# Layer 0 of a four-layer attention kernel: four small matrix-product steps 0.0265 of a beat later in TensorE's order, and the first steps of an item's end 0.06 of a beat later

## What is computed

```python
q = einsum('oc,bct->bot', Wq, x) + bq;  k = ... kv ...;  v = ... kv ...      # bs=8, c=256, t=512
attn = softmax(where(kv_mask, einsum('bhqd,bhdk->bhqk', q / sqrt(d), k), -inf))
mean = einsum('bhqk,bhkd->bhqd', attn, v)
ex2  = einsum('bhqk,bhkd->bhqd', attn, v * v)
std  = sqrt(relu(ex2 - mean * mean))
xn   = (x - mean_t(x)) / sqrt(relu(var_t(x)) + 1e-5)                       # masked, over t
out  = (xn * std + mean) * mask
```

## Time and profile before

| | us |
|---|---|
| median of 3 runs | 3299.74 (3284.89 to 3302.26) |
| the profiled execution's own time | 3297.55 |
| its span, first to last instruction | 3295.8 |
| mean granted clock of TensorE | 0.923 of full speed |
| busy: PE, DVE, ACT, POOL (share of the span) | 2809.2 (85%), 1824.8 (55%), 1338.8 (41%), 881.5 (27%) |

### The profile page before, as it was taken

The page is one execution under the profiler, slowest core; times in us unless marked ns, Lnnn a source line. Parts: engine busy times, 40 slices in busy tenths (PEclk is TensorE's granted clock), DMA queues, the critical chain, the costliest instruction groups (busy, mean ns, idle before and its releaser), DMA issues. The chain is left out here.

```text
span 3295.8 us, 41359 instructions
## 1 busy us (share of the span) xinstructions
PE 2809.2 (85%) x14624; PEld 1317.3 (40%) x14624; DVE 1824.8 (55%) x4498; ACT 1338.8 (41%) x2342; POOL 881.5 (27%) x722
## 2 busy tenths in 40 slices
PE   4988888867999999989999999985668888888895
PEld 1222222224555555556555545542222333333332
DVE  3777777713433433212555665567867776667641
ACT  0566665642333333322333333322215544554562
POOL 1577777752444444310010000001110010101000
PEclk7999999978999999899999999988678899999997
DMA  4444444320002000122323232333333232323210
GB/s 99 102 100 102 102 99 102 67 95 23 27 30 92 28 27 24 65 63 56 67 53 69 57 70 52 70 63 86 67 82 87 69 76 59 89 52 77 66 34 20
DMA packets 182335, 219.93 MB, mean 67 GB/s; under 512 B 40840, under 2 KB 135664, under 8 KB 175984
## 3 DMA queue, kind: packets, MB, share of 16 engines
q1 hardware_dynamic: 170064, 189.74, 25.0%
q0 software_dynamic: 6016, 20.98, 1.9%
q10 hardware_dynamic: 6048, 6.56, 0.6%
HBM read 146.90 MB, written 51.64 MB: 60 GB/s over the span
## 5 line engine op out<-in xcount | busy, mean ns | idle before, releaser
L1260 DVE TENSOR_REDUCE l_M<-PS 128x1 f32<-128x512 f32 x512 | 330.2, 681 | 168.3 <-PE PS L722 167.9
L1480 DVE TENSOR_REDUCE l_M<-PS 128x1 f32<-128x512 f32 x512 | 334.8, 684 | 139.1 <-PE PS L967 136.2
L1199 ACT ACTIVATE l_P<-PS 128x512 f32<-128x512 f32 x512 | 286.3, 599 | 255.3 <-PE PS L977 237.3
L1563 POOL TENSOR_TENSOR l_S<-l_P 128x512 f32<-128x512 f32 x256 | 326.0, 1305 | 62.0 <-ACT l_P L1050 62.0
L1050 ACT ACTIVATE l_P<-PS 128x512 f32<-128x512 f32 x512 | 276.3, 598 | 134.0 <-PE PS L731 133.5
L967 PE MATMUL PS<-l_KS,l_QS 97*128 97x512 bf16 x512 | 205.4, 412 | 102.9 <-DVE l_M L1480 71.7
L1319 DVE TENSOR_REDUCE l1a_M<-PS 128x1 f32<-128x512 f32 x256 | 158.9, 683 | 201.5 <-PE PS L784 201.5
L1164 ACT ACTIVATE l_P<-l_P 128x1024 f32<-128x1024 f32 x128 | 135.3, 1057 | 304.9 <-DVE l_P L1400 304.7
L1386 DVE CUSTOM_DVE_ANT_0 l_JK<-PS,l_MK 128x256 f32<-128x256 f32 x512 | 195.6, 420 | 102.1 <-PE PS L897 99.9
L722 PE MATMUL PS<-l_KS,l_QS 97*128 97x512 bf16 x512 | 202.5, 406 | 57.7 <-DMA l_KS<-l_MB 19.5
L612 PE MATMUL PS<-l_YT,l_w_mlp_w 128*128 128x256 f32 x1024 | 238.6, 390 | 5.2 <-ACT l_YT L1126 5.1
(11 more groups left out here) (244 smaller groups left out, 4639.8 us busy)
## 6 DMA issues: line engine op xcount, KB each, us to landing
l_QS<-q_scratch SPq DMA_DIRECT2D x128, 128.0 KB, 5.6
q_scratch<-l_T SPq DMA_DIRECT2D x96, 128.0 KB
l_QS<-q_scratch SPq DMA_DIRECT2D x32, 384.0 KB, 5.0
k_scratch<-l_T SPq DMA_DIRECT2D x96, 128.0 KB
l_KS<-k_scratch SPq DMA_DIRECT2D x32, 384.0 KB
l_QS<-q_scratch SPq DMA_DIRECT2D x32, 256.0 KB, 5.6
l_KS<-k_scratch SPq DMA_DIRECT2D x32, 256.0 KB
l_RB<-l_recs SPq DMA_DIRECT2D x32, 256.0 KB
```

Of the source, the lines that this page charges most:

```text
L1199: e.activation(t.P[quad % 4][:, m, :], PS[:, COUNTS.bank[st], :], ACT.Exp, scale=0.25).then_inc(q.sem("act.exp", st), 1)
L1260: e.tensor_reduce(t.M[i % 2][:, qt, hd:hd + 1], PS[:, COUNTS.bank[st], :], AX.X, ALU.max).then_inc(q.sem("dve.smax", st), 1)
L1480: e.tensor_reduce(t.M[i % 2][:, qt, hd:hd + 1], PS[:, COUNTS.bank[st], :], AX.X, ALU.max).then_inc(q.sem("dve.smax", st), 1)
L1563: x = e.tensor_tensor(t.S[j % 2][:, m, :], t.P[2 * j % 4][:, m, :], t.P[(2 * j + 1) % 4][:, m, :], ALU.add)
```

## The change

Two due times move, in layer 0 alone. The sums go from 0.8625 + n/4 to 0.889 + n/4. The steps f1 0, f1 1 and f2 go from 0.08, 0.16 and 0.28 to 0.14, 0.22 and 0.34. No instruction is added, removed or altered, no delay in `LATER` is changed, and the order within the rings stays as it was.

```diff
         for n in range(4):
-            out += [(0.51 + n / 4, k("fold", n)), (0.8625 + n / 4, k("sums", n))]
+            out += [(0.51 + n / 4, k("fold", n)), (0.889 + n / 4, k("sums", n))]
...
         if h:
-            out += [(0.08, k("f1", 0)), (0.16, k("f1", 1)), (0.28, k("f2")), (1.2, k("f3", 0)), (1.25, k("f3", 1)),
+            out += [(0.14, k("f1", 0)), (0.22, k("f1", 1)), (0.34, k("f2")), (1.2, k("f3", 0)), (1.25, k("f3", 1)),
```

## The result

The changed kernel takes 3280.5 us in the median (3267.7 to 3289.7) where the kernel before takes 3299.4 on the same chip: a ratio of 0.9943, with a 95% interval of 0.9925 to 0.9960, so 18.8 us less (13 to 25). The prediction was 3281. The profiled execution took 3280.75 us, its span is 3279.0. So the time came out as forecast. Whether it came out so for the reasons given is another question, and the experiments answer it with yes for the largest term and for v 0, and no for proj 1.

A forecast was written before the change was run, and what follows sets the result against it. TensorE was taken as the bound, a pair of beats being set by its own order and then the chain through SP; 13.2 + 3.2 + 2.1 = 18.5 us off gave a median of 3281, 8-in-10 range 3265 to 3300.

The forecast's parts named there:

- Proj 0 in the odd beat: Odd beat: proj 0 1.00 us earlier, its evacuation by DVE 1.20 more; 2.2 us in six beats, 13.2 us.
- SP's queue as almost gapless: Odd beat: SP's DMAs from q's write at 396.29 to RB at 426.79 follow with almost no gap.
- the chain: From the odd beat's proj 0 through SP's DMAs to RB and the maxima; the even beat's stalls hang on it.
- One sign: Even beat: RB should arrive about 2 us earlier after proj 0.
- TensorE's lead and the price of f1: Odd beat: TensorE gains 1.3 us of lead; f1 1 beside POOL costs up to 0.7 us six times, taken as 0.
- V 0: Every beat: the 0.53 us wait for v 0's bank goes; it pays in six even beats, 3.2 us.
- Proj 1: Even beat, at 0.sq: proj 1 goes ahead of sums 2, 0.7 us earlier; 2.1 us, bounds 0 and 4.2.
- The clock did not come back: Rival, chance 0.13: the shorter stall behind 0.sq no longer lowers TensorE's clock; 8.4 us more, 3273.
- ACT held at the sums: Slower rival, chance 0.13: the sums' copy delays ACT's next exponential, 16.0 to 19.2 us over 32 copies; 3316 to 3319.
- The condition named for it: The slower rival decides once ACT's 0.90 us idle time is used up, and if the chain's gain fails too.
- What was costed at nothing: Sums 0 after v 1, f2 behind fold 3, f1 of the last batch: nothing, since no stall hangs on them.

The follow-up runs named there:

- first term alone: Against the kernel before: f1 and f2 moved as in the change, and of the sums only sums 1 of the odd beats; 0.9949, 16.8 us off.
- the sums of the first half alone: Against the kernel before: only sums 1 to 3 of the even beats and sums 0 of the odd ones moved; 0.9959, 13.5 us off.
- Three small delays of due times: Changed kernel with the sums' copy on ACT at 0.05, f3 0 at 1.235 and f3b 0 at 1.335; 0.9861 of before, 3255.8 us.

## Why the prediction was right, and where it was not

*Proj 0 in the odd beat (13.2 us): right.* The steps moved as worked out: proj 0 ahead of sums 1, the evacuation right behind ACT's copy, the third write of q at 6.52 us (6.8 foretold). Tried alone, the term gave 16.8 us (11 to 23), and its pair 2.43 us where 2.2 was foretold. Behind it the reading of SP's queue as almost gapless was too kind: between 396.29 and 426.79 it stands for 9.4 us, in four gaps, but each lies ahead of a DMA that reads what the DMAs just before it wrote, so the gaps move with the chain. One sign was worded wrongly: I wanted RB some 2 us earlier "after proj 0". Of the 2.2 us one is proj 0's own, so from proj 0 only 1.20 can be seen; RB's DMA goes 37.05 us after proj 0 in the mean of the last five odd beats, before 38.16: 1.1 earlier.

The prediction cut a pair in two: from the end of the stall behind 0.sq to the next odd proj 0 by TensorE's own order, and from there to the end of the next such stall by the chain. Both can be read off the starts of these matmuls (means of the same four pairs, us):

| | TensorE's own stretch | the chain's stretch |
|---|---|---|
| before | 21.80 | 59.23 |
| first term alone | 20.88 | 57.72 |
| changed | 20.27 | 58.44 |
| foretold for the change | 1.53 less (sums 1 1.00, v 0 0.53) | 1.55 less (f1 1.20, proj 1 0.35) |
| measured for the change | 1.53 less | 0.79 less |

*TensorE's lead and the price of f1: right.* The stall behind f1 1 came back in part, 0.52 to 0.77 us in the last five odd beats. f1 0 went from 1.07 to 1.46 us there, which I had not counted, f1 1 from 0.68 to 1.20, inside the 0.7 that I had set as its bound. With the first term alone the pair is 2.43 us shorter, so neither has taken anything from it that shows.

*V 0 (3.2 us): right, as far as one execution tells.* TensorE's own stretch is shorter by what was foretold, 1.53 us: 0.92 of it comes with the first term alone, and 0.61 more with the rest of the sums.

*Proj 1 (2.1 us): the stall went as foretold, the gain didn't stay.* The chain's stretch, where it should show, is 0.72 us longer than with the first term alone. Single pairs of either kernel scatter there by 2 to 3 us, so the size is loose; the waits and the rows of proj 1 in 145 to 605 us say where it goes. The changed kernel wins 6.1 us behind 0.sq. It loses 4.6 on the maxima (1.0 to 5.6), 5.6 on proj 1's bank (0.9 to 6.5), and proj 1 takes 4.7 us longer (23.8 to 28.5). The 5.8 won at v 0 belong to the own stretch in the even beats, and in the odd ones to a lead that the chain was foretold to take back. So the step "0.7 us on what sets the end of the stall" failed, with its bound of nothing below: I costed what an earlier proj 1 gives to the square roots, and not what the same step takes away, namely that sums 2 filled the wait for the bank and kept TensorE busy ahead of proj 1. With sums 2 put back, proj 1 is at 615 ns again and no loss of time shows. The medians, 16.8 (11 to 23) and 18.8 us off (13 to 25), are too close to tell.

*The clock did not come back.* The rival let it, for 8.4 us. The stalls behind 0.sq did get shorter, 2.7 to 2.9 us for 3.4 to 4.0, but behind each of the six vals still take 1.93 or 1.94 us, and after the one at 442.06 a small matmul takes 0.61, as in the earlier trace rows. On the other side proj 1 fell to the lower level in three even beats, which no rival had. The mean granted clock of 145 to 552 us, 0.94 for 0.96, is no measure of that: it was 0.93 in the kernel with sums 0 and f2 moved, where proj 1 never fell.

*ACT held at the sums: the mechanism is there, its price isn't.* ACT waits 28.1 us for the sums, but taking nearly three quarters of that away moves the time by less than can be told. The condition named for it, that ACT's idle time is used up, isn't met: ACT still waits 72.5 us for scores in that stretch.

*What was costed at nothing*: sums 0 and f2 were nothing, to within 8 us. The other parts were not tried by themselves.

*The terms do not all add.* The two halves of the change do, within what can be told: 16.5 us for the sums and 6.3 for f1 and f2, 18.8 together. But the first term alone gave 16.8, and the sums of the first half alone 13.5, which share no moved step with it: 30.3 together, where the whole change gave 18.8 (13 to 25). That the sum came out at 18.8 where 18.5 was foretold is luck in part: the term that failed, the first term's 16.8 for 13.2 and what is open below happen to balance, and the pair got 2.32 us shorter where I wanted some 3.

*Open:* why the even beats' sums give 13 to 16 us alone where the rows of before explain 3 to 5. Their two profiled executions show 5.9 and 1.6 us at the end of layer 0. The rest of the measured gain would have to lie in a kernel before that usually ends layer 0 later than 761.9 (the kernel with sums 0 and f2 moved, not faster, ended it at 770.0), or in layers 1 to 3, whose code is the same and whose length in the fourteen profiles runs from 2517.7 to 2541.7 us. The profiled execution of before is a fast one: 3297.55 us, where the median on the chips of these two kernels is 3301.7 and 3307.3. One profile of each cannot tell these apart, and I don't settle on either.

## What to carry to other kernels

When one step is moved ahead of another, ask not only what the moved step reaches sooner but what its neighbour had been filling: here the same swap, with f1 out of its way, paid 16.8 us where the projection begins a chain of DMAs, and nothing that shows where the other work had covered a wait for a bank. And ask what comes to stand behind the passed step: with the sums directly behind proj 0 half of the chain's gain was gone. Terms worked out from separate stalls need not add; try the largest alone before believing the sum. And follow a stall that goes to the place where it turns up next: score bank, then proj 1's bank, then gone. Three small delays of due times took the gain from 18.8 to 45.9 us.

## What the runs showed of the hardware

**The length of a step depends on where POOL is.** In the kernel with f3 0 later, the subtraction 0.f3b takes 1.78 us; one reduction later in DVE's queue it takes 1.18. POOL does the same fold beside it in both. First DVE and POOL of the one, then of the other. POOL's four instructions of a fold are merged into one row; it is given here from windows that end after its first, second and third:

```profile
502.13 1.78 DVE L1289 TENSOR_TENSOR l_EX<-l_EX,l_OUT 128x512 f32<-128x512 f32 x1
505.03 1.77 DVE L1289 TENSOR_TENSOR l_EX<-l_EX,l_OUT 128x512 f32<-128x512 f32 x1
...
502.09 1.26 POOL L1563 TENSOR_TENSOR l_S<-l_P 128x512 f32<-128x512 f32 x1
...
502.09 2.93 POOL L1563 TENSOR_TENSOR l_S<-l_P 128x512 f32<-128x512 f32 x2
...
502.09 4.16 POOL L1563 TENSOR_TENSOR l_S<-l_P 128x512 f32<-128x512 f32 x3
```
```profile
494.80 1.18 DVE L1289 TENSOR_TENSOR l_EX<-l_EX,l_OUT 128x512 f32<-128x512 f32 x1
496.50 1.15 DVE L1289 TENSOR_TENSOR l_EX<-l_EX,l_OUT 128x512 f32<-128x512 f32 x1
...
494.17 1.26 POOL L1563 TENSOR_TENSOR l_S<-l_P 128x512 f32<-128x512 f32 x1
...
494.17 2.94 POOL L1563 TENSOR_TENSOR l_S<-l_P 128x512 f32<-128x512 f32 x2
```

The subtractions of the first kernel end 0.56 and 0.55 us after the end of a POOL instruction (503.91 and 506.80 for 503.35, its first, and 506.25, its third), those of the second kernel 0.55 and 0.54 after one (495.98 and 497.65 for 495.43 and 497.11, the first and the second). In all four the DVE instruction ends 0.54 to 0.56 us after POOL's, so its length goes by how much of POOL's was left when it started: 1.22 us of it for the one of 1.78 us, 0.63 for the one of 1.18. POOL pays as well: its instruction behind one that a subtraction met takes 1.67 or 1.68 us, the first ones 1.26. Over twelve subtractions the difference is 7.3 us of DVE time between the two kernels (21.3 and 14.0 us in 145 to 605). The Trainium skill, page "SBUF — State Buffer", section "Who interferes with whom", has it as a rule, that a DVE instruction with two SBUF inputs contends with a GpSimd instruction that reads SBUF; these rows agree.

**The scatter goes with the granted clock.** In 81 executions of the kernel before, in four sets on three chips, the time falls by 19.6 us for each 0.01 that the mean granted clock is higher (correlation -0.77; -0.63 to -0.85 within the sets). Which of the two drives the other these runs don't show. The whole gain of the change is worth one such step, so a comparison of single executions, profiled ones too, says little about it.
